# A post-norm decoder layer on one core: one new order of the instructions of a pipeline, and tile tables worked out in whole rows, with 71 expert tiles for 72

## What is computed

```python
x = layernorm(x + attention(x))            # 16 heads of 8 features, softmax, Wo, bo
x = layernorm(x + retention(x, ctx, ctx))  # rotated q and k, a decay by head, causal
x = layernorm(x + experts(x))              # top 2 of 8 experts
```

## Time and profile before

| | |
|---|---|
| median of 3 runs | 1089.34 us (1089.06 to 1095.69) |
| the profiled execution | 1096.66 us, its span 1094.8 us |
| PE busy | 867.4 us, 79% of the span |
| DVE / POOL / ACT busy | 821.2 / 646.7 / 625.4 us |

### The profile page before, as it was taken

The page is one execution under the profiler, slowest core; times in us unless marked ns, Lnnn a source line. Parts: engine busy times, 40 slices in busy tenths (PEclk is TensorE's granted clock), DMA queues, the critical chain, the costliest instruction groups (busy, mean ns, idle before and its releaser), DMA issues.

```text
span 1094.8 us, 36565 instructions
## 1 busy us (share of the span) xinstructions
PE 867.4 (79%) x12214; PEld 656.0 (60%) x12215; DVE 821.2 (75%) x2253; ACT 625.4 (57%) x1421; POOL 646.7 (59%) x741
## 2 busy tenths in 40 slices
PE   3555679998989888899986873299999999999700
PEld 2343447666666565666654542188888888888600
DVE  5767689888888888788876544478888888888665
ACT  1231447666666756566665663166666666666445
POOL 0383737888888878788997345134444444444543
PEclk8787889999999999999998775599999999999855
DMA  7242111222222121212212101222222112222176
GB/s 244 45 107 42 19 39 39 61 57 51 55 51 63 48 60 50 56 44 52 56 50 45 40 21 40 68 54 61 58 58 58 58 58 58 58 58 59 36 240 223
DMA packets 145588, 72.31 MB, mean 66 GB/s; under 512 B 75072, under 2 KB 134848, under 8 KB 145472
## 3 DMA queue, kind: packets, MB, share of 16 engines
q1 hardware_dynamic: 125072, 40.66, 15.9%
q0 software_dynamic: 8704, 17.97, 4.9%
q10 hardware_dynamic: 11696, 12.08, 3.5%
HBM read 42.21 MB, written 28.48 MB: 65 GB/s over the span
## 4 chain that ended last, share of the span: by engine, by line
PE 73%; DVE 10%; issue 8%; ACT 3%; DMA 3%; another core or an unknown queue 1%; POOL 1%; ACTq 1%; SPq 0%; DVEq 0%; POOLq 0%
PE QKV L768 9%; PE ST L768 8%; PE ST L639 6%; PE SC L560 6%; PE YY L587 6%; PE SC L796 5%; PE XT L796 5%; PE QKV L548 5%; PE ST L654 3%; PE TR L602 2%; PE XT L611 2%; PE TR L599 2%; DMA prod_ev<-token_halves 2%; PE XT L620 2%; DVE prod_qk L1148 2%
## 5 line engine op out<-in xcount | busy, mean ns | idle before, releaser
L1545 POOL TENSOR_TENSOR prod_ev<-e_sb,q_v 128x512 f32<-128x512 f32 x256 | 296.7, 1192 | 118.6 <-PE YY L587 81.0
L1148 DVE TENSOR_TENSOR prod_qk<-q_v,QKV 128x2048 f32<-128x2048 f32 x64 | 145.7, 2278 | 28.2 <-PE SC L560 19.7
L1592 POOL DMA_INDIRECT token_halves<-w_new,tok_i x144 | 139.8, 971 | 38.2 <-issue 32.1
L1562 POOL DMA_INDIRECT routed_rows<-xe,pos x128 | 127.6, 997 | 30.1 <-issue 27.9
L1034 ACT ACTIVATE prod_qk<-QKV,silu_scale 128x512 f32<-128x512 f32 x144 | 95.7, 686 | 61.9 <-PE QKV L768 60.3
L1447 DVE TENSOR_TENSOR prod_ev<-prod_qk,prod_ev 128x1024 f16<-128x1024 f32 x72 | 88.2, 1225 | 54.5 <-ACT prod_ev L1025 40.5
L410 POOL TENSOR_TENSOR marks<-half_c 128x1 f32<-128x1 f32 x104 | 19.9, 191 | 180.8 <-DVE w_new L1463 159.0
L768 PE MATMUL QKV<-k_t,w_hl 128*128 128x256 f16 x864 | 119.2, 275 | 0.0
L768 PE MATMUL ST<-k_t,w_hl 128*128 128x256 f16 x864 | 118.9, 274 | 0.0
L1473 DVE SCALAR_TENSOR_TENSOR prod_qk<-ST,hid_scale,prod_qk 128x512 f32<-128x512 f32 x144 | 103.7, 744 | 9.0 <-ACT prod_qk L1034 5.3
L921 ACT ACTIVATE q<-XT,tab 128x256 f32<-128x256 f32 x256 | 96.8, 490 | 16.3 <-PE XT L621 16.2
(11 more groups left out here) (171 smaller groups left out, 1828.7 us busy)
## 6 DMA issues: line engine op xcount, KB each, us to landing
w_new<-routed_rows SPq DMA_DIRECT2D x72, 130.0 KB
prod_ev<-token_halves SPq DMA_DIRECT2D x16, 512.0 KB, 5.0
x_sb<-x SPq DMA_DIRECT2D x32, 128.0 KB, 2.4
ctx_sb<-ctx SPq DMA_DIRECT2D x32, 128.0 KB
x_res<-x SPq DMA_DIRECT2D x128, 32.0 KB
head_rows<-o_n SPq DMA_DIRECT2D x32, 128.0 KB
o_t<-head_rows SPq DMA_DIRECT2D x64, 64.0 KB
out<-prod_qk ACTq DMA_DIRECT2D x16, 256.0 KB, 4.0
```

Of the source, the lines that this page charges most:

```text
L1148: eng.tensor_tensor(prod_qk[:, u, :, :].rearrange("p d (i j) -> p d i j", j=NH), q.unsqueeze(3).to_broadcast([P, HD, NH, NH]), k.unsqueeze ...
L1545: ins = eng.tensor_tensor(prod_ev[:, u, q, :, :, 0:HD], e_sb[:, it.slot(2), u, 64 * q:64 * q + 64].rearrange("p (i j) -> p j i", j=4).unsq ...
L1562: eng.indirect_dma_start(out=xs, out_offset=bass.IndirectOffsetOnAxis(ap=pos[:, r, 2 * u + k:2 * u + k + 1], axis=0), in_=xe[:, r, u, k, : ...
L1592: eng.indirect_dma_start(out=halves, out_offset=bass.IndirectOffsetOnAxis(ap=tok_i[:, s, u:u + 1], axis=0), in_=yw[:, s, u, :], in_offset= ...
```

## The change

Two things are changed. The first is the order of each engine's list in stage A, with new lags. PE's `project` stood behind `sums`, `own_heads` and `sums`; it now stands between the first `ret_scores` and the first `scores`. Most lags of PE's and DVE's later operations are larger by one, since the list starts at another point of the cycle, and the waits that depend on the order (`wait_last`) are turned to fit. POOL's two scatters and its norm are elsewhere in its list. The second is the tables: DVE compares all tiles with all experts in one instruction over 8 x 71 elements and sums over experts with a reduction, where before it went from expert to expert; and the last tile, which can never hold rows, is left out.

```diff
-    n_tiles = 2 * n_tok // TILE + n_exp
+    n_tiles = 2 * n_tok // TILE + n_exp - 1
-    PE_LAGS, ACT_LAGS, DVE_LAGS, POOL_LAGS, SP_LAGS = 12, 12, 13, 10, 8
-    CTX_LAG, HEADS_LAG = 8, 8
+    PE_LAGS, ACT_LAGS, DVE_LAGS, POOL_LAGS, SP_LAGS = 13, 12, 13, 11, 9
+    CTX_LAG, HEADS_LAG = 9, 8
-    B_FIRST, B_LAGS = 8, 3
+    B_FIRST, B_LAGS = 7, 3
...
             # PE
+                if it := at(10):
+                    ret_scores(it, 0)
+                if it := at(2):
+                    project(it)
+                if it := at(3):
+                    scores(it, 0)
...
             # DVE: one of its moved entries
-                if it := at(1):
-                    products(it, 0)
+                if it := at(2):
+                    products(it, 0)
...
             # DVE, the tables
+            eng.wait_ge(ov_done, n_duo)
...
-            link(eng.tensor_copy(cum[one, 0:1], n_t[one, 0:1]))
-            for n in range(1, n_exp):
-                link(eng.tensor_tensor(cum[one, n:n + 1], cum[one, n - 1:n], n_t[one, n:n + 1], ALU.add))
-            eng.memset(t_exp[one, :], 0.0)
-            link(eng.memset(t_prev[one, :], 0.0))
-            no = const("tile_no")[one, :]
-            for n in range(n_exp - 1):
-                link(eng.tensor_scalar(t_ge[one, :], no, cum[one, n:n + 1], None, ALU.is_ge))
-                link(eng.tensor_tensor(t_exp[one, :], t_exp[one, :], t_ge[one, :], ALU.add))
-                link(eng.scalar_tensor_tensor(out=t_prev[one, :], in0=t_ge[one, :], scalar=n_t[one, n:n + 1],
-                                              in1=t_prev[one, :], op0=ALU.mult, op1=ALU.add))
+            link(eng.tensor_tensor(by_exp, const("upto")[one, :].rearrange("p (e k) -> p e k", e=n_exp),
+                                   n_t[one, :].unsqueeze(1).to_broadcast([1, n_exp, n_exp]), ALU.mult))
+            link(eng.tensor_reduce(cum[one, :], by_exp, AX.X, ALU.add))
+            link(eng.tensor_tensor(grid, no.unsqueeze(1).to_broadcast([1, n_exp, n_tiles]), along(cum[one, :], n_tiles), ALU.is_ge))
+            link(eng.tensor_reduce(t_exp[one, :], grid[:, 0:n_exp - 1, :].rearrange("p e t -> p t e"), AX.X, ALU.add))
+            link(eng.tensor_tensor(by_tile[:, 0:n_exp - 1, :], grid[:, 0:n_exp - 1, :], along(n_t[one, 0:n_exp - 1], n_tiles), ALU.mult))
+            link(eng.tensor_reduce(t_prev[one, :], by_tile[:, 0:n_exp - 1, :].rearrange("p e t -> p t e"), AX.X, ALU.add))
...
             # POOL
                 if it := at(1):
+                    weighted(it, 0, 1)
+                if it := at(11):
+                    scatter(it, 1)
+                c, d = at(5), at(5 + NORM_GAP)
+                if c or d:
+                    one_over_std(c, d)
...
+                if it := at(1):
                     weighted(it, 1, 0)
                     weighted(it, 1, 1)
                 if it := at(10):
-                    scatter(it, 1)
+                    scatter(it, 0)
                 if it := at(0):
                     weighted(it, 0, 0)
-                    weighted(it, 0, 1)
```

More of the change, by code:

```diff
@@ L712, in step @@
                 spread_max(at)
-                if it := at(7):
-                    residual(it)
+                if it := at(4):
+                    half_over(it)
+                if it := at(11):
+                    ret_values(it)
+                if it := at(10):
+                    queries_across(it)
+                if it := at(11):
+                    own_heads(it)
+                if it := at(4):
+                    quarter_over(it)
+                if it := at(6):
+                    sums(it, 1)
```

192 lines of the change are left out of this document (88 added, 104 removed).

## The result

| | before | after |
|---|---|---|
| median of the runs, us | 1092.5 (4 runs, 1089.1 to 1102.3) | 1114.7 (4 runs, 1113.6 to 1121.3) |
| ratio | | 1.020, 95% interval 1.012 to 1.028 |
| profiled execution, us (its span) | 1096.66 (1094.8) | 1113.58 (1111.4) |

A forecast was written before the change was run, and what follows sets the result against it. PE was taken to bound the kernel, stopping in `project` beside POOL's scatters, with POOL next. Order -20, first steps +4, tables -5.5, tile -4.5 make -26 us: 1089.3 to 1063 us; 8-in-10 range 1048 to 1084.

The forecast's parts named there:

- I take 16.0: Stage A's new step: 16.0 us, between 15.5 (POOL's work) and 16.4 (one short stop left); gain 20 us, bounds 12 and 29.
- What is late next: Stage A: once `project` is whole, POOL limits, with waits through all engines summing to 15.4 us, below 16.0.
- The reading of the stops: PE's `project` in stage A: PE receives instructions late while POOL issues indirect transfers, costing 2.4 us a step.
- the ring of 15.4 us: Stage A: one round of waits through all engines in a step, 14.4 us of operations plus eight handovers.
- the plain step: Stage A before the change: a step at 234.20 taking 17.17 us, where the 16 steps average 17.66.
- Rival 2: Stage A, `own_heads` to `ret_values`: a new wait makes steps exceed 17.9 us; 1100.2 us, or 1107 at 18.3; chance 0.11.
- rival 1: PE in stage A: instruction supply is short wherever scatters are, so stops stay; -6 us, 1083 us; chance 0.14.
- First steps: Start of stage A: DVE waits for the first weights before any products; 4 us lost, at most 4.4.
- Tables: Tables before PE's first tile: 22 linked instructions, 19.4 us down to about 13; 5.5 us gained.
- they must land: Before the first tile: SP's blank rows, issued until 692.5, must land, so no start before 694.5; limits the gain to 5.5 us.
- Tile: Stage B: one tile fewer at 4.53 us each; 4.5 us gained.
- rival 3: Both ends of stage A: new waits of 1.2 us in 13 draining steps, 16 us, 1079 us; equal gain possible; chance 0.11.

The follow-up runs named there:

- scatter_moved: Kernel before with POOL's scatter of the first half moved to that of the second, between the two groups of products; 1136.8 us, ratio 1.038.
- signals: Small separate program: TensorE's groups of narrow matmuls, each with a signal, alone and beside POOL's transfers; beside four transfers three groups were heard 2.1 to 4.0 us late.
- early_two: Changed kernel with DVE's max_of_two moved ahead of chosen_places, positions and one_hot; 1079.9 us, ratio 0.989; on a chip without stops 1105.4 us, 1.057.
- tables_only: Kernel before with only the new tables and 71 tiles, in the old order; 1084.8 us, ratio 0.990, and 1087.0 us, 0.995, on another chip.
- after_again: Changed kernel as it is, measured again on a chip where the kernel before took 1046.0 us; 1135.2 us, ratio 1.085.
- warm_pe: Changed kernel with 16 more matmuls of 256 columns in each TensorE step, between own_heads and quarter_over; 1133.3 us, ratio 1.035.

## Why the prediction was wrong

**The step that failed** is "I take 16.0" for the new step, and under it "What is late next: once `project` is whole, POOL". The reading of the stops was right: `project` is whole, the fast step takes 16.4 us, at the upper bound given, and scatter_moved carries the stops along to wherever the scatters go. But the ring of 15.4 us was summed from durations of single operations, as if they were the same beside anything, and what DVE does ahead of `m_two` while POOL multiplies is not in it: that wait was put at nothing. `xk_b`, `posw` and `oh` cost 0.9 us together where nothing is beside them and 3.8 in the slow step. That pushes `m_two` behind PE's arrival, 1.2 us, and the lower clock adds 2.9. The 16 steps take 311.2 us. The forecast had them at 282.5 - 19 = 263.5, since it let stand what made them longer than the plain step. These 47.7 us are more than the whole miss of the profiled executions (1113.6 for 1070.7, 42.9); the other terms together give some 5 back. By the medians the miss is 52. The trace before already had the price. Had I asked it for the durations (min/median/max in ns) of `oh`, the smallest of these operations, it would have shown one form with thirty-fold spread:

```profile
L1281 DVE TENSOR_TENSOR oh<-tab,ix x64: 161/222/5097, 183.7 to 676.4; 128x16 f32<-128x16 f32 x64
```

I read means and single rows only. In the plain steps it was `oh` that met POOL, 1.1 us for both halves, behind `m_two` and so at no cost; `xk_b` and `posw` met nothing there. The 5.1 us stand at 575 us, in the drain.

**Rival 2** named the right kind (a step over 17.9 us, a wait that closes through DVE and POOL) and gave 1107 at 18.3 us. It looked for the wait at `own_heads` and `ret_values`; it was at `quarter_over`. It is the rival that came true, by another wait than the one it named, and so in part by luck.

**The trade.** The rule of the Trainium skill behind rival 1 ("Runtime: NRT & Kernel Launch", section "Instruction fetch mechanics") would have the stops depend on the number of instructions alone. They follow the scatters' place, and on two chips they are absent with the same program; by that rule alone neither would be. The other kind of stop in `signals`, 128 or 256 recorded matmuls apart, does go by the number of instructions. Getting rid of the stops beside the scatters cost something that the trace before showed only in late steps. With the scatter beside `project` nobody hears late: `project` ends at 255.25 and ACT's copy starts at 255.28. With it beside `sums`, in the step of the earlier trace rows, `sums` ends at 509.40 and POOL goes on at 511.19.

**The other terms.** First steps: 4 us lost by forecast, 6.9 measured, and not for the reason given. The first products are late by 26.03 - 18.35 = 7.7 us, more than the bound of 4.4: the weights were there at 21.43, within the bound, but the 4.4 us of the measurement, which the forecast had as only moved, now stand ahead of the products. Yet early_two has the same delay there and reaches its 13th `project` at 200.1 us, 0.6 later than the kernel before. So this delay is nearly all taken back, and no run shows a loss of 4 us by it. In the changed kernel 5.0 of the 6.9 us are the last period ahead of the 13th `project`, 19.9 us for 14.9: the slow kind of step, already there. Tables: 13 us forecast, 8.0 measured, 12.9 and 12.1 in tables_only; of the 11.4 us gained 7.8 went into a wait for the last scatter, which ends at 718.5, behind the blank rows (715.7): the point that "they must land" was made for the blank rows and not for the scatters. Net 3.6 for 5.5. Tile: 2.7 us of stage B for 4.5, with a slower first tile. The gain of 12.5 us in the drain is in no term of the sum; rival 3 had allowed for one of that size. The tables now begin before the last scatters are out, so the stretches belong together: from the last `project` to the first tile it is 156.3 us for 172.4.

**What stays open**: why PE's instructions and signals are held beside POOL's transfers on some chips and not on others. Each chip was measured at one time only, so whether it is the chip or the moment is not shown either. In every trace the stops and the late signals are either both there or both absent; no run here tells the cause. Nor is it known why the links of the tables are idle for 0.5 us and more in one program and 0.05 in another, or why the clock stayed full in two of the steps with the long wait.

## What to carry to other kernels

Before two engines' lists are re-timed against each other, look in the trace for operations of one form with two durations, and write down what ran beside the long ones; a sum of a ring must take the long value wherever the new order lets them meet, and must have in it every list that runs beside it. An engine that is freed starts earlier, and may do harm there: here an added wait took 2% off. And measure a change of order on more than one chip: the same two kernels differed by 2% on one and by 8.5% on another.

## What the runs showed of the hardware that was not expected

- A DVE operation with two SBUF operands beside POOL's 128x512 multiplications takes 1.19 us for 0.35, one with a single SBUF operand 0.97 for 0.22, one with an operand in PSUM is not touched. In the kernel an operation of 0.42 us was held 5.09 us, through four multiplications in a row.
- While POOL issues indirect transfers (0.96 us each, 0.30 apart), PE's dense narrow matmuls come in groups of about five, and the signals in the stream are heard up to 4.0 us (in the kernel 4.6 us) late. Single matmuls with a wait between them and 512-column ones show neither. On two chips none of this happens, and the kernel before takes 1046 us for 1092 to 1097.
- After a wait of 2.2 us PE's granted clock was 0.61 of full in the mean of the next 6.6 us, so for most of them the lower of its two levels (1.2 and 2.4 GHz). In two steps of after_again the same wait left it at 1.00; a step took 17.6 us there and 20.5 at a mean of 0.83. Where matmuls filled most of the wait (warm_pe, the step at 342.61) it was 1.00.
